# First four batches multiplied with the adapter as the stationary operand, written transposed at once and unsplit

## The reference

```python
w = weight[adapter_ids]                           # (8, 512, 512)
y = jnp.einsum('bij,bkj->bik', x, w)              # y = x w^T
q = y[:, 107:127, :].mean(axis=1)
routing = jax.nn.softmax(q @ router_W.T + router_b, axis=-1)     # (8, 8)
base = y @ W.T + b
t = jnp.einsum('bsd,erd->bser', y, A)             # 8 experts, rank 16
lora = jnp.einsum('bser,eor,be->bso', t, B, routing) * 2.0
out = x + base + lora
```

## Time and profile before

| | |
|---|---|
| median of 3 runs | 71.73 us (71.39 to 71.83) |
| profiled execution, its own time | 72.28 us |
| its span in the trace | 70.6 us |
| TensorE matmul busy | 65.2 us, 92% |
| VectorE, ScalarE busy | 42.0 us, 30.4 us |
| DMA | 15.30 MB, mean 217 GB/s |

### The profile page before, as it was taken

How to read it: one execution, slowest core, us unless ns; L and a number is a source line. 1 busy time by engine, 2 the same in 40 slices (tenths; PEclk the granted TensorE clock), 3 DMA queues, 4 the chain that set the end, 5 groups by cost and what they waited for, 6 DMA issues and landing times.

```text
span 70.6 us, 1064 instructions
## 1 busy us (share of the span) xinstructions
PE 65.2 (92%) x374; PEld 52.2 (74%) x374; DVE 42.0 (59%) x98; ACT 30.4 (43%) x62; POOL 1.2 (2%) x10
## 2 busy tenths in 40 slices
PE   2996987999999999999999999999999999999940
PEld 1331423755699998998998988889999988889920
DVE  1000020748989999949999999994293245138230
ACT  0800032857698996658763693300330444000000
POOL 5100000000000000000000000000000000000000
PEclk9999999999999999999999999999999999999999
DMA  0459899999999999999734204224633000004922
GB/s 0 134 194 393 285 395 388 408 406 412 418 409 409 409 409 406 409 409 411 307 153 102 47 0 104 54 44 110 154 149 149 0 0 0 9 0 134 312 74 74
DMA packets 7590, 15.30 MB, mean 217 GB/s; under 512 B 800, under 2 KB 4000, under 8 KB 7584
## 3 DMA queue, kind: packets, MB, share of 16 engines
q1 hardware_dynamic: 6720, 14.64, 55.6%
q10 hardware_dynamic: 864, 0.59, 3.2%
HBM read 12.08 MB, written 2.10 MB: 201 GB/s over the span
## 4 chain that ended last, share of the span: by engine, by line
PE 80%; DMA 9%; SPq 5%; issue 1%; DVE 0%; DVEq 0%
PE ps_o L594 30%; DMA wc_raw<-in_wcT_dram 9%; PE ps_t L594 8%; PE ps_o L622 8%; PE ps_y L555 5%; PE ps_y L577 4%; PE ps_y L579 4%; PE ps_y L578 4%; SPq L199 3%; PE ps_o L555 3%; PE ps_yT L577 3%; PE ps_yT L578 3%; PE ps_yT L579 3%; PE ps_yT L588 3%; PE ps_y L594 2%; SPq L204 1%
## 5 line engine op out<-in xcount | busy, mean ns | idle before, releaser
L594 PE MATMUL ps_o<-yT_hi,az_hi 128*128 128x256 f32 (+1 forms) x52 | 15.7, 301 | 0.0
L594 PE MATMUL ps_o<-yT_lo,az_hi 128*128 128x256 f32 (+1 forms) x52 | 15.4, 297 | 0.0
L594 PE MATMUL ps_o<-yT_hi,az_lo 128*128 128x256 f32 (+1 forms) x52 | 15.4, 296 | 0.0
L404 DVE TENSOR_TENSOR wc_lo<-wc_raw,wc_hi 128x1024 fp32r<-128x1024 f32 x10 | 11.9, 1215 | 0.1
L594 PEld LDWEIGHTS ps_o<-yT_hi,az_hi 128*128 128x128 f32 x52 | 9.8, 188 | 0.4
L594 PEld LDWEIGHTS ps_o<-yT_hi,az_lo 128*128 128x128 f32 x52 | 9.8, 188 | 0.5
L594 PEld LDWEIGHTS ps_o<-yT_lo,az_hi 128*128 128x128 f32 x52 | 9.8, 188 | 0.3
L309 ACT CAST wc_hi<-wc_raw 128x1024 fp32r<-128x1024 f32 x10 | 10.0, 1050 | 0.0
L476 DVE SCALAR_TENSOR_TENSOR wc_raw<-ps_o,rest_raw,xT_raw 128x256 f32<-128x256 f32 (+1 forms) x12 | 6.2, 542 | 6.0 <-PE ps_o L622 6.0
L555 PE MATMUL ps_y<-wc_raw,xT_raw 128*128 128x512 f32 x16 | 7.4, 597 | 0.5 <-DMA wc_raw<-in_wcT_dram 0.5
L642 PE MATMUL ps_l<-warm 128*128 128x512 bf16 x11 | 4.8, 625 | 1.3 <-DVE warm L481 1.3
(11 more groups left out here) (84 smaller groups left out, 114.6 us busy)
## 6 DMA issues: line engine op xcount, KB each, us to landing
wc_raw<-in_wcT_dram SPq DMA_DIRECT2D x16, 512.0 KB, 12.3
rest_raw<-in_rest_dram SPq DMA_DIRECT2D x2, 512.0 KB, 9.7
xT_raw<-in_xT_dram SPq DMA_DIRECT2D x2, 512.0 KB, 14.3
out_dram<-wc_raw SPq DMA_DIRECT2D x2, 512.0 KB, 3.1
xT_raw<-in_xT_dram SPq DMA_DIRECT2D x3, 256.0 KB, 7.1
yT_raw<-y_turn SPq DMA_DIRECT2D x12, 64.0 KB, 2.1
out_dram<-wc_raw SPq DMA_DIRECT2D x3, 256.0 KB, 2.3
rest_raw<-in_rest_dram SPq DMA_DIRECT2D x1, 278.0 KB, 8.1
```

The lines of the kernel that those rows point to most:

```text
L404: tt(flat(wc_lo[b % 2][:, part_h, :]), flat(wc_raw[:, b, part_h, :]), flat(wc_hi[b % 2][:, part_h, :]).bitcast(F32), ALU.subtract).then_in ...
L594: last = mm(bank, stat[:, n, c, :], yT[mov][:, c].rearrange("p b s -> p (b s)"), start=(start and c == 0 and k == 0), stop=(stop and c == ...
```

## The change

The first four batches are computed raw by `y_across`, with a 128x128 block of the adapter stationary and the 128 tokens of x^T moving, for each of four input chunks c and four output blocks o. That writes y^T directly, to `ps_y` for even batches and `ps_yT` for odd ones. The copies of y, the transposes, the identity, the split of batch 1's second half and the split of batch 3 go. The stored order of the features in `az` becomes the plain one, and `turn` now reads its bank with a step of four elements. `project_t(0)` and `logits(0)` stand between the two halves of batch 2.

```diff
-    RAW = 3
+    RAW = 4
...
+        def yT_bank(b):
+            return ps_yT if b % 2 else ps_y
...
-            def copy_y(b, bank):
-                act.wait_ge(y_done, b + 1)
-                copy(y_sb.rearrange("p (c t k) -> p c t k", c=C, k=NT),
-                     bank[:].rearrange("p (c k t) -> p c t k", c=C, k=NT)).then_inc(y_copied, 1)
...
-            hi_x1()
-            copy_y(0, ps_y)
-            for c in range(HALF, C):
-                hi_wc1(c)
             hi_yT(0)
-            copy_y(1, ps_o[3])
+            hi_yT(1)
             hi_az(0)
-            hi_yT(1)
-            hi_x(3)
             hi_az(1)
-            copy_y(2, ps_y)
             hi_az(2)
...
-            hi_wc(3)
             hi_az(4)
             hi_x(4)
             hi_wc(4)
-            copy_y(3, ps_y)
             hi_x(5)
...
             def turn(b):
-                dve.wait_ge(y_done, b + 1)
+                dve.wait_ge(y_done, b - RAW + 1)
                 nc.vector.transpose(y_turn[b % 2].rearrange("p k c s -> p c k s"), y_bank(b)[:].rearrange(
-                    "p (c k s) -> p c k s", c=C, k=NT)).then_inc(y_turned, 1)
+                    "p (c s k) -> p c k s", c=C, k=NT)).then_inc(y_turned, 1)
...
-            lo_x1()
-            for c in range(HALF, C):
-                lo_wc1(c)
             lo_yT(0)
             lo_az(0)
             lo_yT(1)
...
-            lo_x(3)
...
-            lo_wc(3)
...
-            def y_raw(b, c, bank):
+            def y_across(b, c):
                 if c == 0:
                     pe.wait_ge(x_arrived(b), 16)
+                    if b >= 2:
+                        pe.wait_ge(q_ready, b - 1)
                 if c % HALF == 0:
                     pe.wait_ge(wc_in[b][c // HALF], 16)
-                last = mm(bank[:], xT_raw[:, b, c, :], wc_raw[:, b, c, :], start=(c == 0), stop=(c == C - 1))
+                for o in range(C):
+                    last = mm(yT_bank(b)[:, o * S:(o + 1) * S], wc_raw[:, b, c, o * P:(o + 1) * P], xT_raw[:, b, c, :],
+                              start=(c == 0 and o == 0), stop=(c == C - 1 and o == C - 1))
                 if c == C - 1:
-                    last.then_inc(y_done, 1)
+                    last.then_inc(yT_done, 1)
...
-            for c in range(C):
-                y_raw(0, c, ps_y)
+            for b in range(2):
+                for c in range(C):
+                    y_across(b, c)
             for c in range(HALF):
-                y_raw(1, c, ps_o[3])
-            pe.wait_ge(ident_ready, 1)
-            transpose_y(0)
-            for c in range(HALF, C):
-                y1_split(c, ps_o[3])
-            for c in range(C):
-                y_raw(2, c, ps_y)
-                if c == 0:
-                    transpose_y(1)
+                y_across(2, c)
+            pe.wait_ge(az_lo_ready, 1)
+            project_t(0)
             pe.wait_ge(ones_ready, 1)
             logits(0)
-            pe.wait_ge(az_lo_ready, 1)
-            project_t(0)
+            for c in range(HALF, C):
+                y_across(2, c)
             pe.wait_ge(az_lo_ready, 2)
             base(0, 0)
-            transpose_y(2)
...
             for c in range(C):
-                y_split(3, c)
+                y_across(3, c)
             pe.wait_ge(az_lo_ready, 5)
             base(0, 3)
-            transpose_y(3)
             lora(0, 3)
```

More of the change, by code:

```diff
@@ L66, in adapter_lora_kernel @@
         b_lo = sb("b_lo", [P, D], F32R)
-        ident = sb("ident", [P, P])
         ones = sb("ones", [P, P])
@@ L262, in _ @@
         def _(pool):
-            nc.gpsimd.memset(ident[:], 0.0).then_inc(ident_zeroed, 1)
             nc.gpsimd.memset(mask[:], LORA_SCALE).then_inc(mask_set, 1)
             nc.gpsimd.memset(ones[:], 1.0).then_inc(ones_ready, 1)
-            pool.wait_ge(ident_zeroed, 1)
-            nc.gpsimd.affine_select(out=ident[:], in_=ident[:], compare_op=ALU.not_equal, fill=1.0, base=0,
-                                    pattern=[[-1, P]], channel_multiplier=1).then_inc(ident_ready, 1)
             pool.wait_ge(mask_set, 1)
@@ L295, in hi_yT @@
                     act.wait_ge(yT_done, b + 1)
-                    copy(yT_home(yT_hi, yT4_hi, b), per_chunk(ps_yT[:])).then_inc(yT_hi_ready, 1)
+                    copy(yT_home(yT_hi, yT4_hi, b), per_chunk(yT_bank(b)[:])).then_inc(yT_hi_ready, 1)
                 else:
@@ L310, in hi_wc @@
                         .then_inc(wc_hi_ready, 1)
[L312 to L318, removed]
             def exponent(g):
@@ L331, in hi_tsT @@
                                          scale=rout[:, i:i + 1]).then_inc(tsT_hi_ready, 1)
-            act.wait_ge(ident_ready, 1)
+            act.wait_ge(mask_ready, 1)
             act.dma_start(flat(xT_raw[:, 0]), xT0[0]).then_inc(x_arrived(0), 16)
@@ L362, in _ @@
             hi_wc(5)
-            act.wait_ge(y_done, 5)
+            act.wait_ge(y_done, 5 - RAW)
             hi_x(6)
@@ L368, in _ @@
             hi_yT(4)
-            act.wait_ge(y_done, 6)
+            act.wait_ge(y_done, 6 - RAW)
             hi_x(7)
@@ L421, in lo_yT @@
                 if b < ON_PE:
-                    tt(lo, per_chunk(ps_yT[:]), hi.bitcast(F32), ALU.subtract).then_inc(yT_lo_ready, 1)
-                    nc.vector.tensor_reduce(sums, per_chunk(ps_yT[:])[:, :, Q_START:Q_END], AX.X, ALU.add)\
+                    tt(lo, per_chunk(yT_bank(b)[:]), hi.bitcast(F32), ALU.subtract).then_inc(yT_lo_ready, 1)
+                    nc.vector.tensor_reduce(sums, per_chunk(yT_bank(b)[:])[:, :, Q_START:Q_END], AX.X, ALU.add)\
                         .then_inc(q_ready, 1)
@@ L572, in y_split @@
                 if c == 0:
+                    if b == RAW:
+                        pe.wait_ge(q_ready, b - 1)
                     pe.wait_ge(xT_lo_ready, b - RAW + 1)
@@ L581, in y_split @@
                     last.then_inc(y_done, 1)
[L583 to L586, removed]
-                for c in range(C):
-                    last = nc.tensor.transpose(ps_yT[:, c * S:(c + 1) * S], y_sb[:, c * P:(c + 1) * P], ident[:])
-                last.then_inc(yT_done, 1)
             def products(n, bank, yT, start, stop):
@@ L729, in contraction_first @@
         return np.ascontiguousarray(m)
-    def turned(m):
-        axis = m.ndim - 3
-        m = m.reshape(*m.shape[:axis], 4, 32, *m.shape[axis + 1:])
-        return np.ascontiguousarray(np.swapaxes(m, axis, axis + 1)).reshape(*m.shape[:axis], P, *m.shape[axis + 2:])
     az = np.concatenate([a.reshape(e * r, d), w]).reshape(c + 1, P, d)
-    consts = np.concatenate([turned(contraction_first(rw)).reshape(P, c * e), np.broadcast_to(rb.reshape(1, e), (P, e)),
+    consts = np.concatenate([contraction_first(rw).reshape(P, c * e), np.broadcast_to(rb.reshape(1, e), (P, e)),
                              bias.reshape(c, P).T], axis=1)
     xT = contraction_first(x).reshape(nb, P, c, s)
-    azT = turned(contraction_first(az)).reshape(c + 1, P, d)
+    azT = contraction_first(az).reshape(c + 1, P, d)
     bT = b.transpose(0, 2, 1).reshape(e * r, d)
```

16 lines of the change are left out of this document (removed).

## The result

The changed kernel took 73.02 us (median of 6, 72.70 to 74.23), the kernel before on the same chip 71.83 (median of 6, 71.39 to 72.98). The ratio is 1.0159, 95% interval 1.0122 to 1.0195: 1.1 us slower. In a second series beside other kernels it was 1.0192 (1.0127 to 1.0258).

A forecast was written before the change was run, and what follows sets the result against it. Bound: landing of wc(1,0), then gapless TensorE matmul records and a short tail. Removed work -11.31, raw records +10.94, restart +0.24, new wait +0.95 gave +0.82 us on 71.73: 72.5 us predicted, 8-in-10 range 71.5 to 73.8.

The forecast's parts named there:

- three signs of being wrong: Pitch outside 0.110 to 0.118, a second gap before 31 us, or work after batch 4 changing its length.
- The pitch: Time per raw 128-column record on TensorE in batches 1 to 3: 0.114 us, 96 records making 10.94 us.
- Rivals 2 and 3: First: weight loads partly exposed, +4.05 us at pitch 0.15, chance 0.12. Second: records at the router's 0.07 pitch, -1.95 us, chance 0.10.
- The new wait: TensorE ahead of project_t(0) waits for batch 1's low y^T: 0.68 us idle plus 0.27 restart, +0.95 us.
- Batch 0: Its 32 records, from 6.57 to 10.49 us, end before batch 1's adapter lands at 10.91: no cost.
- The restart of batch 1: TensorE's first record after waiting for batch 1's adapter costs more than a pitch: +0.24 us remains.
- The sum of the early stretch: Change between 11.05 us and batch 4's start at 31.10: +0.82 us, batch 4 starting at about 31.9.
- Batch 3: Its split, 2.72 us, and transposes, 0.44, go; 32 raw records at 0.114 us come, counted only within the sum.
- Batch 4 on: nothing.: From batch 4 TensorE comes 0.8 us later, VectorE no later, and the work keeps its length: no cost.
- rival 4: VectorE's turn, reading PSUM with a step of four, takes 2.84 us and becomes the bound: +3.3 us, chance 0.05.
- slack of batch 7's y^T: Late in the kernel, batch 7's y^T has 0.8 us to spare, plus 0.82 from TensorE's later arrival.
- SP's queue as unchanged: Among the edits costed at nothing: SP's queue stays as it was.

The follow-up runs named there:

- e3: Changed kernel with its 64 raw matmuls of 128 columns as 16 of 512, x^T stationary, writing y for y^T; ratio 1.0076 to the kernel before.
- e2: Changed kernel with project_t(0) and logits(0) moved behind all of batch 2; ratio 1.0248 to the kernel before.
- e6: Changed kernel with project_t(0) and logits(0) behind three of batch 2's four chunks, not two; ratio 1.0136 to the kernel before.
- e1: Changed kernel run again unedited, for its trace and as partner of the runs beside it; ratio 1.0192 to the kernel before.
- e4: Changed kernel with batch 3 split, copied and transposed as in the kernel before; ratio 1.0053 to the kernel before.
- e5: Changed kernel with 44 warm-up matmuls of 128 columns in place of 11 of 512; no ratio, median 73.99 us.
- e11: Same kernel as e5, run again for its time; ratio 1.0117 to the kernel before.
- e8: Kernel of e4 with 30 warm-up matmuls of 188 columns in place of 11 of 512; ratio 1.0163 to the kernel before.

## Why the prediction was right in its time, and where it failed

The median I forecast was 72.5, the measured one 73.02, inside the range; the difference of 1.14 to 1.37 us stands against my +0.82. Of my three signs of being wrong, one came: work after batch 4 changed its length.

- **The pitch.** Forecast 0.114, between 0.110 and 0.118. Measured 3.59 / 32 and 3.57 / 32 = 0.112. The quarter of the wide raw record (0.1075) was a better neighbour than the split record (0.118), and the transposes (0.110), which I had set aside as another mode, were the nearest. e3 confirms the price of the shape, 0.14 us per batch. Rivals 2 and 3 are out. The Trainium skill (TensorE: Matmul & The Clock Gate, section "The mechanism") states that a weight load overlaps matmuls in flight only when it targets other row groups. By that rule the pitch would have been some 0.22 by my estimate; the measured 0.112 contradicts it again.
- **The new wait.** Forecast 4.19 us from the end of batch 1 to the end of `project_t(0)` (2.50 + 0.27 + 1.42); measured 14.39 to 18.59, 4.20. That it fits to the hundredth is partly luck: the way through ScalarE and VectorE took 2.60 and not 2.50, the product with its restart 1.60 and not 1.69. What I did not see is that the order after it is no freer: e2 shows the wait cannot be bought off with more work in front, since the router then takes its place; with three chunks, e6, neither waited.
- **Batch 0.** Forecast: no cost, since its records would end at 10.49, before batch 1's adapter lands at 10.91. This step failed. Both times came from the one trace of before, and the two landings vary: batch 0's first half landed at 6.47 us there and at 6.86 in the changed kernel, batch 1's at 9.9 to 11.1 in the 13 traces. In the changed kernel batch 0 ended 0.55 us after that landing: +0.41.
- **The restart of batch 1.** Forecast +0.24. In the changed kernel batch 0 ends at 10.80 us, after batch 1's adapter has landed, and batch 1 follows without a break. e1 and e6 show some of the restart, 3.74 and 3.81 us for 3.59. A term of 0 to 0.24.
- **The sum of the early stretch.** +0.32 measured from the start of batch 1, against +0.82: the pitch 0.16 less, the restart 0.24 less, and the two base products after batch 2 in 2.73 us where I had kept 2.84. So TensorE came to batch 4 at 31.17 us, 0.07 later than before, and not 0.8 later at 31.9.
- **Batch 3.** It was inside the sum but deserved to be named: 3.57 raw for 3.16 split and transposed. e4 gets 0.4 us back by undoing this part alone.
- **"Batch 4 on: nothing."** This step failed. VectorE and ScalarE were indeed no later, and the turn took 0.71 us with its step of four as without (rival 4 is out):

```profile
L391 DVE STREAM_TRANSPOSE y_turn<-ps_y x2: 707/712/716, 34.0 to 44.5; 128x512 f32<-128x512 f32 x2
```

But 0.58 us came in there. I counted the slack of batch 7's y^T as 0.8 us, and 0.82 more for TensorE's lateness, which did not come, and looked only for compute that could use it up. Its landing used it up: the block landed at 52.55 us and not at 51.16 as before, 1.39 later, and 1.39 less 0.8 is the 0.58. The cause was a transfer of TensorE's instructions, moved by the larger number of records onto the last block. I had listed SP's queue as unchanged and not asked about the instruction queue at all. So the time came out near the forecast by errors of opposite sign, which is luck: pitch, restart and base products 0.51 too dear, batch 0's 0.41 and the late 0.58 missing; 0.82 - 0.51 + 0.41 + 0.58 = 1.30.

## What to carry to other kernels

Bound a new shape of matmul from every record near it, and do not set the nearest one aside by its name. A landing time read from one trace is one draw: where a stage is said to be covered by a load, see what the sum becomes when the load lands half a microsecond earlier or later. When a change adds instructions to an engine, look at where the instruction queue's transfers fell before, and at which small, late DMA they may land on. A wait covered by independent work is only gone if what hangs on the covered step has slack of its own.

## What the runs showed of the hardware that I had not expected

- TensorE's instructions came by DMA in pieces of 16 KB during the run, three in eleven traces and four in e5 and e11, each 0.9 to 1.5 us long. When one met the last 64 KB block move, that move landed 3.8 to 4.2 us after its issue instead of 2.3 to 2.5 (changed kernel, e1, e2, e6, e8).
- A raw float32 matmul of 128 columns followed at 0.112 us per record while its 128x128 weight load lasted 0.19 us in the trace; 32 such records in a row took 3.57 us, against 3.43 for the same work in 8 records of 512 columns (e3), so at most 0.005 us of each load is exposed.
- VectorE's transposing read of PSUM cost the same, 0.71 us for 128x512, with a step of one element and of four.
